# Padding rows written in blocks during the steps, with four smaller edits, in a fused attention and expert kernel

## The reference

```python
mod = (silu(c) @ wmod).reshape(16, 6, 1, 128)          # sa, ca, ga, sb, cb, gb
h = layernorm(x) * (1 + ca) + sa
x = x + ga * attention(h)                              # causal linear attention, 16 heads of 8
h = layernorm(x) * (1 + cb) + sb
x = x + gb * experts(h)

# experts: top 2 of 8 experts for each token
h = rmsnorm(s @ W_in.T, in_norm_w)
logits = h @ Wr.T
gates = softmax(logits[top2 of (logits + expert_bias)])
out = sum over e of gates[:, e] * rmsnorm((silu(h @ Wg[e].T) * (h @ Wu[e].T)) @ Wd[e].T, enorm_w[e])
s_hat = rmsnorm(out, out_norm_w) @ W_out.T
```

## Time and profile before

| what | value |
|---|---|
| median of three timed executions | 414.87 us |
| the profiled execution, its own time | 414.08 us |
| its span, first to last instruction | 412.2 us |
| mean granted clock of TensorE | 0.939 |
| PE busy | 354.4 us, 86% of the span |
| DVE busy | 323.8 us, 79% |
| ACT busy | 291.9 us, 71% |
| POOL busy | 236.5 us, 57% |
| DMA traffic | 35.68 MB, mean 87 GB/s |

### The profile page before, as it was taken

One profiled execution on the slowest core, in us unless ns is written; L12 is line 12 of the kernel. 1 busy time (PEld: TensorE's weight loads), 2 busy tenths in 40 slices (PEclk: granted clock), 3 DMA queues, 4 the chain that ended last, 5 costly groups with the idle time before them and its releaser, 6 DMA issues.

```text
span 412.2 us, 12923 instructions
## 1 busy us (share of the span) xinstructions
PE 354.4 (86%) x3757; PEld 307.9 (75%) x3758; DVE 323.8 (79%) x1037; ACT 291.9 (71%) x814; POOL 236.5 (57%) x211
## 2 busy tenths in 40 slices
PE   7899998999999999982069999999999999990464
PEld 4788886888888888861049889989899898980443
DVE  5568998899999999976928887878778877870696
ACT  5465776888888888546328878778778787773595
POOL 0665585688888888856341645454454445453441
PEclk9999998999999999995559999999999999997698
DMA  7899000000000000111423333333333333213833
GB/s 217 356 368 363 2 28 26 8 30 27 26 26 26 26 26 26 34 40 51 131 40 54 68 71 70 62 71 60 64 64 71 60 69 65 57 34 110 351 94 94
DMA packets 46563, 35.68 MB, mean 87 GB/s; under 512 B 36291, under 2 KB 42070, under 8 KB 45750
## 3 DMA queue, kind: packets, MB, share of 16 engines
q1 hardware_dynamic: 41862, 25.40, 21.9%
q0 software_dynamic: 4544, 9.39, 7.0%
q10 hardware_dynamic: 128, 0.53, 0.5%
HBM read 18.69 MB, written 13.47 MB: 78 GB/s over the span
## 4 chain that ended last, share of the span: by engine, by line
PE 70%; DVE 10%; ACT 6%; issue 5%; DMA 4%; POOL 1%; SPq 1%; DVEq 0%; ACTq 0%; POOLq 0%
PE bank L1474 12%; PE bank L1723 9%; PE bank L1724 8%; PE bank L1725 8%; PE bank L1738 4%; PE bank L1740 4%; PE bank L1554 4%; PE bank L1739 4%; PE bank L1497 3%; DVE prod L960 2%; ACT junk L835 2%; DVE wmaxs L1056 1%; PE bank L1561 1%; DMA cst<-consts 1%; PE bank L1581 1%
## 5 line engine op out<-in xcount | busy, mean ns | idle before, releaser
L559 POOL DMA_INDIRECT expert_rows<-late,to_place x78 | 79.2, 1015 | 85.9 <-DVE late L1333 73.3
L1723 PE MATMUL bank<-late,w_hi 128*128 128x256 f16 x312 | 86.4, 277 | 15.1 <-DMA late<-dispatched 13.7
L1724 PE MATMUL bank<-late,w_hi 128*128 128x256 f16 x312 | 86.4, 277 | 0.0
L1725 PE MATMUL bank<-late,w_lo 128*128 128x256 f16 x312 | 86.3, 276 | 0.0
L518 POOL TENSOR_TENSOR kv<-kv,v 128x1024 f32<-128x1024 f32 x32 | 67.7, 2134 | 32.0 <-ACT kv L686 32.0
L1319 DVE SCALAR_TENSOR_TENSOR kv<-bank,uscale,kv 128x512 f32<-128x512 f32 x78 | 58.5, 750 | 30.4 <-ACT kv L777 18.6
L536 POOL DMA_INDIRECT dispatched<-rows,pos x64 | 67.3, 1051 | 25.7 <-issue 18.2
L1474 PE MATMUL bank<-cst,kv 128*128 128x128 f32 x576 | 74.3, 279 | 0.0
L777 ACT ACTIVATE kv<-bank,descale 128x512 f32<-128x512 f32 x78 | 53.6, 687 | 24.0 <-PE bank L1725 20.1
L1474 PEld LDWEIGHTS bank<-cst,kv 128*128 128x128 f32 x576 | 68.9, 193 | 0.3 <-issue 0.2
L783 ACT ACTIVATE kv<-kv 128x512 f16<-128x512 f32 x78 | 48.8, 625 | 16.8 <-DVE kv L1319 12.3
(11 more groups left out here) (233 smaller groups left out, 733.2 us busy)
## 6 DMA issues: line engine op xcount, KB each, us to landing
late<-wguT SPq DMA_DIRECT2D x1, 4096.0 KB, 17.8
late<-expert_rows SPq DMA_DIRECT2D x1, 2064.0 KB, 10.9
gates_bc<-gate_rows SPq DMA_DIRECT2D x1, 2048.0 KB, 6.9
wd<-wdT SPq DMA_DIRECT2D x1, 2048.0 KB, 25.0
out<-kv SPq DMA_DIRECT2D x16, 128.0 KB, 1.8
late<-dispatched SPq DMA_TRANSPOSE x78
expert_rows<-late,to_place POOLq DMA_INDIRECT x78
late<-expert_rows SPq DMA_DIRECT2D x1, 1032.0 KB, 6.5
```

The source lines that it names most:

```text
L559: pool.indirect_dma_start(ybuf, bass.IndirectOffsetOnAxis(ap=to_place[:, s, r:r + 1], axis=0), yt[:, s, r, :], None).then_inc(y_scat[s], 16)
L1723: mm(o, w_hi[:, w], hi, start=True, stop=False)
L1724: mm(o, w_hi[:, w], lo, start=False, stop=False)
L1725: last = mm(o, w_lo[:, w], hi, start=False, stop=True)
```

## The change

1. **Padding in blocks.** SyncE no longer waits for `tail`. During the steps it writes padding over whole blocks of 256 rows in all 8 regions at once, 17 blocks, the first two when TensorE has projected k and v of three batches, the last when 14 are done. A block writes 8 x 256 rows of 516 bytes from `filler` to `hbuf` in one transfer; two may be under way. The semaphores `padded[0]` and `padded[1]` count even and odd blocks. A batch b can only write rows below 256 (b + 1) of a region, so VectorE's `positions` of batch b waits for block b. The eight writes at the end, `tail`, `tail_f` and two VectorE operations are gone. SyncE loads the row numbers first and waits for scatters and padding after that.
2. **One turning transfer per tile**, 256 rows x 256 f16 values, instead of two.
3. **Late turn of the weight maxima.** Still in step 7, TensorE turns the maxima before the second chunk of the second half, VectorE's `weight_power` follows its products of the second half, the spreading matmul stands at the end of TensorE's step, into a column of another bank (`FFN`), after the ranks are used, and `weight_scale` at the end of VectorE's step.
4. **Filling matmuls.** `keep_busy(bank, n)` issues n matmuls of 512 bf16 columns whose result nobody reads: 5, 13, 3 and 12 in the drain, 24 after the totals, 8 after the last scatter has landed and before the first tile.
5. **Weight columns by bytes.** `columns_of` takes the same columns from a view of the arrays as bytes, with the register's factor doubled.

```diff
-            sp.wait_ge(tail_done, 1)
-            tail_regs = [sp.alloc_register(f"tail{e}") for e in range(E // 2)]
-            sp.load(tail_regs, tail[0:1, 0:E // 2])
-            for e in range(E // 2):
-                row = sp.snap(tail_regs[e], min_val=0, max_val=E * REGION - R)
-                sp.dma_start(hbuf[bass.ds(row, R), :].rearrange("(p j) w -> p (j w)", p=16),
-                             filler[e * R:(e + 1) * R, :].rearrange("(p j) w -> p (j w)", p=16)).then_inc(filled, 16)
-            sp.wait_ge(scattered[0], 16 * NT * K * (B // 2))
-            sp.wait_ge(scattered[1], 16 * NT * K * (B // 2))
-            sp.wait_ge(filled, 16 * (E + 1))
+            regions = hbuf[0:E * REGION, :].rearrange("(e s p j) w -> s p e (j w)", e=E, p=16, j=R // 16)
+            padding = filler[0:E * R, :].rearrange("(e p j) w -> p e (j w)", p=16, j=R // 16)
+            for s in range(REGION // R):
+                sp.wait_ge(kv_ps, 3 + s * (B - 5) // B)
+                if s >= 2:
+                    sp.wait_ge(padded[s % 2], 16 * (s // 2))
+                sp.dma_start(regions[s], padding).then_inc(padded[s % 2], 16)
             sp.wait_ge(table_done, 1)
...
-                for half in range(2):
-                    sp.dma_start(hT3[:, s, half], hbuf16[bass.ds(row, R), half * D:(half + 1) * D],
-                                 transpose=True).then_inc(slot_ld[s], 16)
+                sp.dma_start(hT3[:, s], hbuf16[bass.ds(row, R), 0:2 * D], transpose=True).then_inc(slot_ld[s], 16)
...
                 sp.load(row_regs, tile_row[0:1, bass.ds(TURN * i, TURN)])
+                if not again_turn(i):
+                    sp.wait_ge(filled, 16)
+                    for s in range(2):
+                                sp.wait_ge(padded[s], 16 * ((REGION // R + 1 - s) // 2))
+                    sp.wait_ge(scattered[0], 16 * NT * K * (B // 2))
+                    sp.wait_ge(scattered[1], 16 * NT * K * (B // 2))
...
 (ScalarE: its four padding writes between the chunks of projection_high are gone)
...
             def positions(b, p, n):
                 dve.wait_ge(ohs_done, b + 1)
+                dve.wait_ge(padded[p], 16 * n)
...
                 if att is not None:
+                    running_products(att, 1)
                     if scale:
-                        weight_scale(att)
-                    running_products(att, 1)
+                        weight_power(att)
...
                     count_chosen(rb, rp)
+                if scale:
+                    weight_scale()
...
-                    if scale and cc == 1:
-                        if t == 0:
-                            pe.wait_ge(wmax_done, 1)
-                            mm(MAX_ROW, wmax[:], ident, start=True, stop=True)
-                        else:
-                            pe.wait_ge(wpow_done, 1)
-                            mm(MAX_ALL, ones[0:1, :], wpow_row[:], start=True, stop=True)
+                    if scale and t and cc == 1:
+                        pe.wait_ge(wmax_done, 1)
+                        mm(MAX_ROW, wmax[:], ident, start=True, stop=True)
...
                     head_sums(att, 1)
+                if scale:
+                    pe.wait_ge(wpow_done, 1)
+                    pe.wait_ge(ohs_done, rte[0] + 1)
+                    mm(MAX_ALL, ones[0:1, :], wpow_row[:], start=True, stop=True).then_inc(wall_ps, 1)
+
+            def keep_busy(bank, n):
+                for _ in range(n):
+                    mm(bank[:].rearrange("p (a n) -> p a n", n=P), ones16[:],
+                       ones16[:].unsqueeze(1).to_broadcast([P, 4, P]), start=True, stop=True)
...
                 head_sums(b15, 1)
+                pe.wait_ge(cum_used[1][1], B)
+                keep_busy(CUM[1], 5)
                 spread(*b15)
                 ranks(*b13)
                 turn(*b14)
                 project(*b15)
                 into_experts(*b14)
+                keep_busy(CUM[1], 13)
                 ranks(*b14)
                 turn(*b15)
+                keep_busy(CUM[1], 3)
                 into_experts(*b15)
+                keep_busy(CUM[1], 12)
                 ranks(*b15)
...
             mm(TOTAL, ones16[:], oh_all[:, B, NT * K, :], start=True, stop=True).then_inc(total_ps, 1)
+            keep_busy(CUM[0], 24)
...
+            def columns_of(w, e, per_expert, at):
+                return w.bitcast(U8)[:, bass.ds(e * (2 * per_expert) + 2 * at, 2 * P)].bitcast(F16)
...
             pe.wait_ge(moe_ld, 32)
+            pe.wait_ge(scattered[0], 16 * NT * K * (B // 2))
+            pe.wait_ge(scattered[1], 16 * NT * K * (B // 2))
+            keep_busy(CUM[0], 8)
             turn_of_tiles(0, first=True)
```

More of the change, by code:

```diff
@@ L755, in _ @@
             pipelined(act, step, drain)
-            for c in range(2):
-                projection_high(c)
-            act.wait_ge(tail_done, 1)
-            tail_regs = [act.alloc_register(f"act_tail{e}") for e in range(E // 2)]
-            act.load(tail_regs, tail[0:1, E // 2:E])
-            for e in range(E // 2, E):
-                row = act.snap(tail_regs[e - E // 2], min_val=0, max_val=E * REGION - R)
-                act.dma_start(hbuf[bass.ds(row, R), :].rearrange("(p j) w -> p (j w)", p=16),
-                              filler[e * R:(e + 1) * R, :].rearrange("(p j) w -> p (j w)", p=16)).then_inc(filled, 16)
-            for c in range(2, DN):
+            for c in range(DN):
                 projection_high(c)
@@ L1720, in gate_up @@
                     o = (G, U)[part][h][:, c * R:(c + 1) * R]
[L1721 to L1725 removed]
+                    wh, wl = (columns_of(w[:], e, F, part * E * F + (h * (FC // 2) + c) * P) for w in (w_hi, w_lo))
+                    mm(o, wh, hi, start=True, stop=False)
+                    mm(o, wh, lo, start=False, stop=False)
+                    last = mm(o, wl, hi, start=False, stop=True)
                 last.then_inc((g_ps, u3_ps)[part], 1)
```

36 lines of the change are left out of this document (14 added, 22 removed).

## The result

The changed kernel takes 410.01 us (median of 6 runs, 408.69 to 414.30) against 414.88 for the kernel before (6 runs beside them, 413.69 to 416.79): ratio 0.9888, interval 0.9859 to 0.9917. A second set of six gave 410.61 against 415.6: 0.9861 (0.983 to 0.9891). So it is about 5 us faster: the direction is the forecast's and the time lies in its range, but the gain is about half of the forecast 9.4. The profiled execution took 408.69 (span 406.8). Slow executions, among them one of 1252 us in e4 and one of 482 in e8, are left out of the ratios and intervals and kept in the medians.

What follows compares the result with a forecast made beforehand. It took TensorE as the busiest engine, losing time at step 7, in the drain and before the experts. Terms summed to -9.0 us: 414.08 to 405.1, or 405.9 beside the median; 405.5 was taken, range 401.5 to 411.5.

Steps and rivals of the forecast that it cites:

- A: Step 7: the late turn of the weight maxima removes TensorE's 1.85 us wait; -1.2 us, bounds 0 and -3.0.
- the two distances: Sign around step 7: successive kv projections would stand 12.8 and about 11.3 us apart.
- B: Last scatter: lands earlier without padding writes beside it, row numbers loaded before the waits; -3.1 us, bounds -2.2 and -3.3.
- third rival: Last scatter's landing held up by HBM, not the padding writes, leaving 0.4 of the gain: 408.2 us; chance 0.08.
- C: Before the first expert tile: one turning transfer for two brings the rows earlier; -0.8 us, bounds 0 and -1.4.
- D: Start of the experts: fillers keep the clock high for the first 24 matmuls; -2.3 us, bounds 0 and -2.7.
- second rival: The clock falls again before the tiles (407.8 us), or also before the 13 drain fillers (411.7); chance 0.15 together.
- E: Drain of the pipeline: fillers let three matmul groups run at the high clock; -1.3 us, bounds -1.6 and +2.6.
- F: Steps: 17 padding blocks land in time and VectorE's wait for them costs nothing; price 0.
- The sign named for being wrong: In the steps: the forecast is wrong if steps after 40 us are longer than 10.31 us.
- first rival: Steps: padding traffic stretches GpSimd's scatter issues from 0.958 to 1.683 us, +31 us, so 436; chance 0.12.
- G: Expert loop: byte-wise weight columns may shorten TensorE's 0.22 us gaps at eight turns; -0.3 us, bounds 0 and -1.8.

Runs made afterwards that it cites:

- e4: Changed kernel with padding blocks paced, each from the fifth on waiting for the scatters of four batches before: 409.2 us, ratio 0.9847.
- e8: Changed kernel with early, then paced padding blocks, 30 and 13 fillers before the experts, 4 in step 7, 48 before the last stage: 409.81 us, ratio 0.9858.
- e7: Changed kernel with the turn of the weight maxima back where the kernel before had it: 410.84 us, ratio 0.9875.
- e5: The kernel before, unchanged, profiled a second time: 415.79 us.
- e1: The changed kernel, unchanged, run and profiled a second time: 410.61 us, ratio 0.9861.
- e2: Changed kernel with the padding written at the end, as in the kernel before: 412.84 us, ratio 0.9937.
- e6: Changed kernel with two turning transfers a tile instead of one: 409.78 us, ratio 0.9842.
- e17: Changed kernel with two turning transfers a tile, on a third kind of chip (kernel before 428.0 us): 423.29 us, ratio 0.9911.
- e3: Changed kernel without its filling matmuls, all six `keep_busy` calls out: 411.05 us, ratio 0.9901.
- e11: Changed kernel with weight columns addressed in two-byte words as before, on a chip where the kernel before takes 431.3 us: 421.33 us, ratio 0.9763.
- e13: The changed kernel, unchanged, on a chip where the kernel before takes 431.9 us: 421.31 us, ratio 0.9802.

## Why the prediction was right in direction and too large

The steps of the working, one by one; "found" is from the table's means unless said otherwise.

- **A, -1.2: this step failed.** Found: -0.1 (24.15 in e7 and 24.09 in e5 to 24.05), and no difference shows in the times (ratios 0.9875 in e7, 0.9861 and 0.9888 for the changed kernel). That the two distances came out as forecast was luck: their sum is what the kernel before has too where its clock holds. The stall of 1.85 us was real, but its step's excess of 4.0 us was not its price: e5 has the same stall and 24.09 us. The excess held a fall of the clock that comes in some executions and not in others, in this kernel or that (e1, e2 and e6 have it a step later, with the wait gone). "The projection about 1.5 us earlier" was 0.32: `den`, which I had named as what is late next, stands behind the same reductions (2.34 us for two). Of the bounds, "0 (VectorE alone sets the step)" was the answer.
- **B, -3.1: right.** Landing 5.17 to 2.26 us, -2.9, and the register load mostly hidden. The third rival is out: with the padding back at the end the landing is 4.72 again.
- **C, -0.8: right in most executions.** Rows 1.36 + 2.28 = 3.64 us behind the first issue; one transfer takes 2.64 to 2.85 in six profiles and 4.25 in e1. The times (e6) don't show it. The term left out that the second transfer also widens the gap behind the fillers (D) and delays the second tile (e17). B and C together: 5.76 us over the profiles of the changed kernel, e1, e4 and e7, against 9.22, so -3.45 of 3.9.
- **D, -2.3: right while the gap before the tile is short.** -2.0 over the same four (7.04 against 9.02): 6.6 to 6.8 us in three and 8.02 in e1, where the second rival held. Waits of 0.93 to 1.95 us behind the fillers left the clock at 2.4 GHz, those of 2.54 and 2.71 did not.
- **E, -1.3: right.** -1.1 and -1.7 against the two profiles of before; 1.8 by e3. All fillers fitted, and GpSimd's scatters now leave hardly more to win.
- **F, 0: failed, +0.65.** "The wait costs nothing" held for the blocks, which landed in time, and not for two other things. The steps are 10.36 us instead of 10.30 in every profile with the wait on these chips, 0.4 us over the stretch. And a block holds up scatters, for which ScalarE waits two batches later (1.54 us in front of L607 instead of 1.12): "still 10 us ahead of its buffer's reuse" was wrong, since the reuse comes 7.0 us after the start of the last scatter, so that a landing of 5.2 us is 1.8 ahead and one of 7.3 is late. "At 310 GB/s a block takes 3.4 us" was wrong too: the median landing of a block is 6.7 us in e1 and 5.5 to 6.6 in the other profiles that tell it. The stall came in two of five profiles (0.4 us and, in e1, 0.1). The sign named for being wrong, steps longer than 10.31, came. The first rival's form, every scatter stretched, did not come: 954 and 958 ns are as before. The Trainium skill, DMA: Bandwidth & Descriptors, section on queues, rings and completion order, has an engine alternate between rings by packets; the trace agrees: landings longer, issues the same, save for that one 0.05 us.
- **G, -0.3: nothing** (151.36 to 151.30; e11).

Sum found: -0.1 - 3.45 - 2.0 - 1.4 + 0.65 = -6.3, where -9.0 stood; A is 1.1 of the shortfall, F 0.65, B and C 0.45, D and G 0.3 each, and E gives 0.1 back. The medians have -4.9. The other 1.4 us are as much as the pairs of the table differ by in the first and last stage (+0.8 and +0.6), where the change has no work; with 0.4 to 2.6 us between two executions there, that they are chance is not shown. The forecast was summed against one execution that was late before step 8, and term A took that for a cost of the kernel.

Open: what sets the first stage's 26.5 to 29.9 us; why fillers that save 3 us in the traces save 0.4 to 1.7 in the times; whether one transfer is what saves some 6 us on two chips, where fillers, late turn and one transfer were only taken out together.

## What to carry over

Before a stall is priced at the excess of its step, look for the same step in a second execution: a granted clock that fell there may be chance, and what stands on the other engines behind the same producer sets what is left. A transfer hidden in a loop is not free because it lands in time: look at what is under way when it is released, and count the time to a buffer's reuse from rows of the trace instead of from the number of steps. Fillers keep the clock only if the gap behind them is short in the slow case of the transfer as well, so size them for that one: here waits up to 1.95 us kept it, and waits of 2.54 and 2.71 lost it.

## What the runs showed of the hardware

- Chips differ by 3 to 4% on the same kernel (415.6, 428.0, 431.9 us) at nearly equal durations of instructions; the difference lies mostly between them. The one group that differs in total by over 2 us between the changed kernel's first profile and e13 is GpSimd's scatters of the experts, 1058 against 1133 ns in the mean of 78. GpSimd's own issue time in the expert loop (230 to 360 us; in total, times, longest), the changed kernel on two chips:

```profile
POOL expert_rows L558 <- issue: 10.8, 33, 1.0
```

```profile
POOL expert_rows L558 <- issue: 23.4, 47, 1.0
```

- The granted clock was 0.50 from 10 us on in five of ten profiles on the chips of 415 us, e1 and e5 of the changed kernel and before among them, and 1.00 in the others; with six fillers at 6 us it held to 15 us in both profiles, as it did in four of the eight without them on the other chips.
- One turning transfer of 256 rows x 256 values landed in 2.64 to 2.85 us six times and once in 4.25, at the same place of the program.
- A scatter started up to 0.1 us before a block of 1.06 MB of padding took 5.1 to 7.3 us to land in the changed kernel's profile, against a median of 2.4 in the profile of before, and its issue stayed at 0.96 us.
